# Turning the gathered rows in one piece, a group ahead, in the first stage of a four-layer graph network

## The chip, the cores and the metric

One Trainium2 chip, one of its cores. The time is device time in microseconds (us) of one execution of the whole program; shown are the median of several runs and one profiled execution. Engines: PE is TensorE, PEld its weight loads, DVE VectorE, ACT ScalarE, POOL GpSimd, SP the engine that issues most transfers.

## What is computed

A graph of 12,500 nodes with 32 features and 412,500 edges sorted by destination. Four layers, each followed by a layer norm over x plus the layer's output:

```python
# layer 0: an edge network, averaged over the edges of a node, then a node network
h = concatenate([x[src], edge_attr_16], axis=1)        # 48 wide
h = maximum(h @ w1a + b1a, 0.0)                        # 96 wide
h = h @ w1b + b1b
agg = segment_sum(h, dst) / maximum(count, 1)
x = layernorm(x + (maximum(concat([x, agg]) @ w2a + b2a, 0) @ w2b + b2b))
# layer 1: ten steps of normalised propagation, f = 0.9 * (A f) + 0.1 * f0
# layer 2: x = layernorm(x + A x)
# layer 3: messages from node features, edge directions and a radial network, summed by dst
```

A is the matrix of how many edges run from a node to another. The kernel builds it once, in the first stage, as counts in 8-bit floats, and layers 1 and 2 multiply by it.

## The kernel before

The nodes stand in NB = 98 blocks of 128, the edges in NG = 324 groups of 1280 (G = 10 tiles of 128). The change touches one stage alone, the function `edges_and_adjacency`, which does two things interleaved on all engines.

The first is layer 0's edge network. For each group POOL gathers the 1280 source rows with ten indirect DMAs into one of NX = 6 buffers `xin`, laid out edges by features. PE transposes each 128x32 tile into the bank `xt_ps` (features by edges, on 32 partitions), ACT copies that to `xt`, where the 16 edge attributes and a row of ones already stand below it. PE multiplies by `w1a` in two halves of five tiles (`hidden`), ACT applies the Relu to each half out of the same bank `h_ps`. Then, for each block of nodes that the group's destinations reach (the "visits", 1.3 a group on average, because the edges are sorted), DVE writes a one-hot matrix and PE sums the ten tiles into `e_visit_ps` with ten matmuls. The block numbers, first and end, are read on PE and on DVE from a table in SBUF (`blocks`, two `value_load`).

The second is the count matrix A. It is made in NQ = 56 quarters; in each, 56 pairs of node windows. A "pair" is four matmuls: for each of two windows one into `a_ps` (one of two banks, by the pair's parity) and one into `degree_ps`, from one-hot matrices `hot_hi` and `hot_lo` that DVE writes in batches of eight windows, four pairs, into two buffers. ACT casts each pair from `a_ps` to the fp8 `image`, and PE waits for `a_taken` of the pair two before. SP stores an image of a quarter in seven parts; ACT may write over an image when all seven of the older quarter are stored (`image_stored`). Once in a quarter PE also folds an image (49 matmuls) as a check.

After two quarters of pairs alone, a loop of 54 turns does a quarter of pairs and six groups (m = 0 to 5) each. DVE does 3, 2, 2, 3, 2, 2 batches ahead of a group's visits (`BATCHES`), so PE and ACT have 12, 8, 8, 12, 8, 8 pairs to place in a group. The order in a group is written out by hand, in the same order on PE and ACT: `STEPS_PAIRS` says how many pairs follow each step. Before the change the steps are: transposes of four tiles, of four, of two (`SUB`), each followed by 2 pairs; hidden half 0; hidden half 1; then 6 or 2 pairs; then the visits. Semaphores: `xt_ready` and `xt_evac` count three per group, POOL gathers into a buffer again when the three transposes of the group that used it are done, and SP loads the attributes of the group after next when the hidden matmuls (`h_ready`) and DVE's part of the visits (`group_read`) of this group are done.

Of the kernel before, what the change touches and what calls it, by code (L numbers as in the profile page):

```python
# [31 lines left out]
P = 128  # L32
# [60 lines left out]
def await_alone(eng, passed, sem, value):  # L93


    eng.wait_ge(sem, value)
    eng.sem_inc(passed, 1)
# [355 lines left out]
        nc.scalar.sqrt(var[:], var[:]).then_inc(root_ready, 1)  # L453


STEPS_PAIRS = ((2, 2, 2, 0, 6, 0), (2, 2, 2, 0, 2, 0))
BATCHES = (3, 2, 2, 3, 2, 2)
SUB = [(0, 4), (4, 4), (8, 2)]
HT = 5
M1 = DH + 1  # L460

# [1 line left out]
def edges_and_adjacency(nc, k, s):  # L463
# [16 lines left out]
    ones = sb("ones_col", [P, 1], F32, s)  # L480
    answer = sb("answer", [1, 4], F32, s)

    xt_ps = pb("xt_ps", [D, 512], F32, s)
    degree_ps = pb("degree_ps", [P, 512], F32, s)
    h_ps = pb("h_ps", [EP, 512], F32, s)
    visit_ps = pb("e_visit_ps", [M1, 512], F32, s)
# [18 lines left out]
    def blocks(eng, g):  # L505
        first = eng.value_load(k.table[0:1, 0, bass.ds(g, 1)], min_val=0, max_val=NB - 1)
        end = eng.value_load(k.table[0:1, 1, bass.ds(g, 1)], min_val=1, max_val=NB)
        return first, end

    with nc.Block() as block:  # L510

        @block.gpsimd
        def _(pool):
            with pool.Fori(1, NG // NX) as i:
                for m in range(NX):
                    await_alone(pool, k.passed_pool, k.idx_loaded[m], i * 16 + 16)
                    await_alone(pool, k.passed_pool, xt_ready, i * (3 * NX) + (3 * m + 3 - 3 * NX))
                    gather_group(k, pool, m)

        @block.sync  # L520
# [42 lines left out]
        @block.tensor  # L563
        def _(pe):
            def pairs(q, at, count):

                for l in range(at, at + count):
                    bank = l % 2
                    batch = l // 4
                    if l % 4 == 0:  # L570
                        pe.wait_ge(hot_ready, q * BPQ + (batch + 1))
                    pe.wait_ge(a_taken, q * QP + (l + 1))
                    for v in range(2):
                        w = l % 4 * 2 + v
                        lo = hot_lo[batch % 2][:, w, :]
                        counts = nc.tensor.matmul(a_ps[:, bank, v * WC:(v + 1) * WC], lo, hot_hi[batch % 2][:, w, :], start=True, stop=True)  # L576
                        mm = nc.tensor.matmul(degree_ps[:, 0:WC], lo, hot_hi[batch % 2][:, w, :], start=False, stop=False,  # L577
                                              skip_group_check=True)
                    counts.then_inc(a_ready, 1)
                    if l % 4 == 3:  # L580
                        mm.then_inc(hot_used, 1)

            def fold(q, n):

                pe.wait_ge(a_taken, q * QP + (QP + 2))
                await_alone(pe, k.passed_pe, folds_read, q + 1)
                for j in range(NB // 2):
                    strip = slice(j % 4 * D, (j % 4 + 1) * D)
                    mm = nc.tensor.matmul(check_ps[strip, 0:2 * QW], folded[:], image[:, n, 2 * j:2 * j + 2, :].bitcast(FP8),
                                          start=(j < 4), stop=(j >= NB // 2 - 4), tile_position=(0, j % 4 * D))  # L590
                mm.then_inc(folds_done, 1)

            def transposes(g, m, b):
                t0, tn = SUB[b]
                pe.wait_ge(xt_evac, g * 3 + (b + 1))
                for t in range(t0, t0 + tn):
                    mm = nc.tensor.transpose(xt_ps[:, (t - t0) * EP:(t - t0 + 1) * EP], xin[m][:, t, :], k.ident[:])  # L597
                mm.then_inc(xt_ready, 1)

            def hidden(g, m, b):  # L600
                pe.wait_ge(xt_evac, g * 3 + (3 + b))
                pe.wait_ge(h_evac, g * 2 + (b + 1))
                for t in range(HT):
                    mm = nc.tensor.matmul(h_ps[:, t * DH:(t + 1) * DH], xt[:, m % 2, (b * HT + t) * EP:(b * HT + t + 1) * EP], w1a[:],  # L604
                                          start=True, stop=True)
                mm.then_inc(h_ready, 1)

            def visits(g, m):
                pe.wait_ge(h_evac, g * 2 + 3)
                first, end = blocks(pe, g)  # L610
                with pe.Fori(first, end):
                    v = pe.snap(count, min_val=0, max_val=NG * NB)
                    pe.wait_ge(onehot_ready, v + 1)
                    pe.wait_ge(added, v + 2)
                    for j in range(G):
                        mm = nc.tensor.matmul(visit_ps[:, 0:P], hid[m % 2][:, j, :], view(onehot[:], (v % 2) * (G * P) + j * P, [[1, P]]),  # L616
                                              start=(j == 0), stop=(j == G - 1))
                    mm.then_inc(product_done, 1)
                    pe.reg_add(count, count, 1)

            def group(g, twos, m, turn, q, at):

                run = STEPS_PAIRS[BATCHES[m] == 2]
                pe.wait_ge(gathered[m], turn * (16 * G) + 16 * G)
                transposes(g, m, 0)
                pairs(q, at, run[0])
                transposes(g, m, 1)
                at += run[0]
                pairs(q, at, run[1])
                transposes(g, m, 2)  # L630
                at += run[1]
                pairs(q, at, run[2])
                at += run[2]
                pe.wait_ge(loaded[m % 2], twos * 32 + 32)
                hidden(g, m, 0)
                pairs(q, at, run[3])
                hidden(g, m, 1)
                at += run[3]
                pairs(q, at, run[4])
                at += run[4]  # L640
                visits(g, m)
                pairs(q, at, run[5])
                return at + run[5]

            pe.wait_ge(weights_loaded, 32)
            pe.wait_ge(zero_ready, 1)
            pe.wait_ge(folded_ready, 1)
            count = pe.alloc_register("e_visits_pe")
            pe.reg_mov(count, 0)
            nc.tensor.matmul(degree_ps[:, 0:WC], zero[0:1, 0:P], zero[0:1, 0:WC], start=True, stop=False, skip_group_check=True)  # L650
            nc.tensor.matmul(visit_ps[:, 0:P], zero[0:1, 0:M1], zero[0:1, 0:P], start=True, stop=True).then_inc(product_done, 1)
            pairs(0, 0, QP)
            pairs(1, 0, QP)
            fold(0, 0)
            with pe.Fori(0, NQ - 2) as u:
                at = 0
                for m in range(NX):
                    at = group(u * NX + m, u * (NX // 2) + m // 2, m, u, u + 2, at)
                    if m == 1:
                        odd = pe.snap(u % 2, min_val=0, max_val=1)  # L660
                        with pe.If(odd < 1):
                            fold(u + 1, 1)
                        with pe.If(odd > 0):
                            fold(u + 1, 0)
            fold(NQ - 1, 1)
            pe.wait_ge(verdict_ready, 1)
            nc.tensor.matmul(check_ps[0:1, 0:2], ones[:], verdict[:], start=True, stop=True).then_inc(verdict_turned, 1)

        @block.scalar
        def _(act):  # L670
# [8 lines left out]
                    nc.scalar.copy(view(image[:], h * (NB * QW) + 4 * l, [[QW, NB], [1, 4]]).bitcast(FP8),  # L679
                                   view(a_ps[:], l % 2 * 512, [[1, NB], [NB, 4]]), saturate=False).then_inc(a_taken, 1)  # L680

            def turned(g, m, b):
                t0, tn = SUB[b]
                act.wait_ge(xt_ready, g * 3 + (b + 1))
                nc.scalar.copy(xt[0:D, m % 2, t0 * EP:(t0 + tn) * EP],  # L685
                               xt_ps[:, 0:tn * EP]).then_inc(xt_evac, 1)

            def hidden(g, m, b):
                act.wait_ge(h_ready, g * 2 + (b + 1))
                nc.scalar.activation(hid[m % 2][:, b * HT:(b + 1) * HT, 0:DH], view(h_ps[:], 0, [[DH, HT], [1, DH]]),  # L690
                                     ACT.Relu).then_inc(h_evac, 1)

            def group(g, m, q, h, at):

                run = STEPS_PAIRS[BATCHES[m] == 2]
                turned(g, m, 0)
                pairs(q, h, at, run[0])
                at += run[0]
                turned(g, m, 1)
                pairs(q, h, at, run[1])  # L700
                at += run[1]
                turned(g, m, 2)
                pairs(q, h, at, run[2])
                at += run[2]
                hidden(g, m, 0)
                pairs(q, h, at, run[3])
                at += run[3]
                hidden(g, m, 1)
                pairs(q, h, at, run[4] + run[5])
                return at + run[4] + run[5]  # L710

            act.wait_ge(ones_ready, 1)
            pairs(0, 0, 0, QP)
# [1037 lines left out]
```

## Time and profile before

| what | value |
|---|---|
| median of 3 runs | 17071.12 us (17070.09 to 17088.16) |
| the profiled execution's own time | 17098.35 us |
| its span, first to last instruction | 17096.5 us |
| mean granted clock of TensorE | 0.891 |
| the changed stage, from the first transpose to the last visit | about 346 to 5775 us, 324 groups |

The page cuts the span into 40 slices of 427 us; slices 2 to 14 are the stage. A line of grouped instructions has the engine, the operation, what it writes and reads, how often, then busy time and mean ns of one, then the engine's idle time just before them and what ended it. "issue" means that nothing in the profile was waited for. In a timeline each line is a start, a length and in brackets the idle time before. A matmul's modelled end is late, so that consecutive ones overlap in the rows; from start to start is what one costs. A 4-byte matmul stands as two records.

### The profile page before, as it was taken

The numbers are of one execution on the slowest core, as the hardware profiler recorded it, in microseconds if no ns is written. First come the engines' busy times: TensorE is split into PE (matmuls) and PEld (weight loads), VectorE is DVE, ScalarE is ACT, GpSimd is POOL, SyncE is SP. The second block draws the span as 40 slices with busy tenths as digits, with TensorE's granted clock in tenths as the row PEclk, the third lists the DMA queues.
The fourth block names the chain that finished last, engine by engine and source line by source line (L and its number), as shares of the span: only waits on it lengthen the run. The fifth ranks groups of instructions, "written<-read, shape, count | busy, mean of one in ns | idle before, by whom it ended". The sixth has DMA issues, their size and how long they took to land. (4 is left out here: it accounts for less than half of the span.)

```text
span 17096.5 us, 397550 instructions
## 1 busy us (share of the span) xinstructions
PE 14417.9 (84%) x141860; PEld 9526.3 (56%) x141861; DVE 8838.1 (52%) x13201; ACT 5006.3 (29%) x10225; POOL 7476.6 (44%) x8530
## 2 busy tenths in 40 slices
PE   3888888888888769999999999878888888888887
PEld 2667677667766535555555555544444444444444
DVE  6555555555555421111011110128888888888888
ACT  2333333333333200000000000004444444444444
POOL 4555555555555100000000000017777777777776
PEclk9877777777777669999999999989999999999999
DMA  2111111111111039998999999861111111111111
GB/s 85 45 44 43 42 45 43 44 43 45 43 44 43 29 142 345 341 343 337 340 342 339 341 341 342 316 223 30 31 31 31 31 31 31 31 30 31 31 31 29
DMA packets 1140415, 2191.40 MB, mean 128 GB/s; under 512 B 399083, under 2 KB 506087, under 8 KB 1138759
## 3 DMA queue, kind: packets, MB, share of 16 engines
q1 hardware_dynamic: 928851, 2062.78, 33.7%
q0 software_dynamic: 210496, 113.01, 4.6%
q8 instruction: 837, 13.71, 0.3%
q14 instruction: 231, 1.89, 0.0%
HBM read 2002.85 MB, written 172.28 MB: 127 GB/s over the span
## 5 line engine op out<-in xcount | busy, mean ns | idle before, releaser
L1413 POOL DMA_INDIRECT m_src<-x_after_layer,m_idx x3240 | 3105.1, 958 | 6785.4 <-DMA m_idx<-in_src 5668.7
L1171 PE MATMUL p_prod<-a_slot,f_parts 128*32 128x448 fp8e4 x90552 | 4474.7, 360 | 392.0 <-issue 343.6
L175 POOL DMA_INDIRECT l_xin<-in_x,l_idx x3240 | 3068.0, 947 | 2476.5 <-DMA l_idx<-in_src 1268.3
L1171 PEld LDWEIGHTS p_prod<-a_slot,f_parts 128*32 128x32 bf16 x90552 | 2566.6, 99 | 2247.1 <-issue 586.7
L1544 PE MATMUL radial_ps<-radial_w,radial_hidden 128*128 128x384 f32 x6480 | 2459.6, 512 | 401.2 <-DVE m_products L1683 209.1
L1549 PE MATMUL m_visit_ps<-m_products,m_onehot 128*128 128x288 f32 x8420 | 2349.9, 427 | 456.2 <-DVE m_products L1702 239.2
L1264 DVE TENSOR_TENSOR agg<-agg,p_back 128x224 f32 x154 | 59.7, 388 | 4463.0 <-PE p_back L1185 4463.0
L1549 PEld LDWEIGHTS m_visit_ps<-m_products,m_onehot 128*128 128x128 f32 x8420 | 1599.7, 193 | 1226.9 <-issue 640.5
L1544 PEld LDWEIGHTS radial_ps<-radial_w,radial_hidden 128*128 128x128 f32 x6480 | 1140.0, 191 | 1630.2 <-DVE m_products L1683 759.5
L616 PE MATMUL e_visit_ps<-e_onehot,e_hidden 128*97 x8420 | 1581.8, 368 | 541.2 <-issue 480.2
L750 DVE TENSOR_TENSOR hot_hi<-window_hi,number_ps 128x1568 bf16<-128x1568 f32 x784 | 1399.9, 1786 | 1175.2 <-PE degree_ps L577 1114.1
L616 PEld LDWEIGHTS e_visit_ps<-e_onehot,e_hidden 128*97 128x97 f32 x8420 | 1472.4, 239 | 671.4 <-issue 671.4
L1683 DVE TENSOR_TENSOR m_products<-radial_ps,m_features 128x256 f32<-128x256 f32 x4860 | 1745.4, 415 | 0.0
L1224 ACT COPY turned<-p_prod 128x896 f32<-128x896 f32 x154 | 139.6, 906 | 5004.3 <-PEq L1178 5004.3
L576 PE MATMUL a_ps<-hot_hi,hot_lo 128*128 128x196 bf16 x6272 | 1461.7, 282 | 97.0 <-DVE hot_lo L752 88.3
L1516 ACT ACTIVATE m_difference<-m_nodes,m_dst 128x128 f32 x3240 | 982.1, 388 | 1884.7 <-PEq L1569 1884.7
L679 ACT CAST a_image<-a_ps 128x392 fp8e4<-128x392 f32 x3136 | 1404.6, 483 | 266.4 <-PE a_ps L576 236.5
L577 PE MATMUL degree_ps<-hot_hi,hot_lo 128*128 128x196 bf16 x6272 | 1459.7, 281 | 0.0
L1679 DVE TENSOR_TENSOR m_products<-radial_ps,m_features 128x512 f32<-128x512 f32 x1620 | 1113.1, 687 | 414.6 <-PE radial_ps L1544 296.4
L1499 ACT ACTIVATE radial_hidden<-edge_w,radial_w 64x1280 f32<-64x1280 f32 x324 | 874.7, 2700 | 1041.4 <-DMA m_unit<-edge_directions 904.1
L685 ACT COPY xt<-xt_ps 32x512 f32<-32x512 f32 (+1 forms) x972 | 491.0, 505 | 2315.4 <-PE xt_ps L597 2182.2
L604 PE MATMUL h_ps<-w1a,xt 49*128 49x96 f32 x6480 | 984.9, 302 | 213.7 <-ACT e_hidden L690 213.7
(197 smaller groups left out, 11894.1 us busy)
## 6 DMA issues: line engine op xcount, KB each, us to landing
a_slot<-multiplicity_digit SPq DMA_DIRECT2D x1078, 1568.0 KB, 9.3
multiplicity_digit<-a_image SPq DMA_DIRECT2D x392, 392.0 KB
edge_w<-in_edge_weight SPq DMA_DIRECT2D x324, 320.0 KB
l_xin<-in_x,l_idx POOLq DMA_INDIRECT x3240
m_src<-x_after_layer,m_idx POOLq DMA_INDIRECT x3240
xt<-in_edge_attr SPq DMA_DIRECT2D x324, 80.0 KB
edge_directions<-rel_unit SPq DMA_DIRECT2D x12, 675.0 KB, 3.8
m_unit<-edge_directions SPq DMA_DIRECT2D x324, 25.0 KB
```

The source lines that it names most:

```text
L175: pool.indirect_dma_start(k.xin[m][:, j, :], None, k.io["x"], bass.IndirectOffsetOnAxis(k.idx[m][:, j:j + 1], 0)).then_inc(k.gathered[m], 16)
L576: counts = nc.tensor.matmul(a_ps[:, bank, v * WC:(v + 1) * WC], lo, hot_hi[batch % 2][:, w, :], start=True, stop=True)
L577: mm = nc.tensor.matmul(degree_ps[:, 0:WC], lo, hot_hi[batch % 2][:, w, :], start=False, stop=False, skip_group_check=True)
L616: mm = nc.tensor.matmul(visit_ps[:, 0:P], hid[m % 2][:, j, :], view(onehot[:], (v % 2) * (G * P) + j * P, [[1, P]]), start=(j == 0), stop= ...
L679: nc.scalar.copy(view(image[:], h * (NB * QW) + 4 * l, [[QW, NB], [1, 4]]).bitcast(FP8), view(a_ps[:], l % 2 * 512, [[1, NB], [NB, 4]]), s ...
L750: tt(hot_hi[b % 2][:], view(k.window_hi[:, bass.ds(at, WB)], 0, [[1, WB], [0, WC]]), view(numbers, 0, [[0, WB], [1, WC]]), ALU.is_equal)
L1171: mm = nc.tensor.matmul(view(prod[m][rows, w, :], 0, [[QW, 2], [1, QW]]), source[:, h * HH + j, r * D:(r + 1) * D], slots[h][:, 2 * w:2 * ...
L1413: pool.indirect_dma_start(src[m][:, j, :], None, k.x3_d, bass.IndirectOffsetOnAxis(idx[m][:, j:j + 1], 0)).then_inc(gathered[m], 16)
L1544: mm = nc.tensor.matmul(r_ps[:, half, t, 0:RD], hid[m][:, b * RB + t, :], w2[:], start=True, stop=True)
L1549: mm = nc.tensor.matmul(view(v_ps[:], (v % 3) * 512, [[U + 1, D], [1, U + 1]]), onehot[one][:, j, :], view(prod[m][:], j * PW + FIRST, [[R ...
L1679: tt(view(prod[m][:], t0 * PW + 1, [[PW, RB], [RW, 2 * U], [1, 2 * U]]), view(r_ps[:], at, [[512, RB], [2 * U, 2 * U], [1, 2 * U]]), view( ...
L1683: mul = tt(view(prod[m][:], t0 * PW + LONG + o * U * RW + 1, [[PW, RB], [RW, U], [1, 2 * U]]), view(r_ps[:], at + 4 * U * U, [[512, RB], [ ...
```

## The change

In words: ten transposes of one 128x32 tile each, in three steps, become three transposes, of four, four and two tiles side by side (128, 128 and 64 columns of `xin`), into one bank of 128 partitions; tile t0 + place of each comes out on the 32 partitions of `place`. ACT brings them to `xt` with four copies, one for each set of 32 partitions, of 3, 3, 2 and 2 tiles. They are done for the group ahead: transposes of group g + 1 stand before the visits of g, its copies on ACT after the second run of pairs; only for m = 0, the first group of a turn, they stand at the group's own start. PE reads the block numbers after hidden half 0 and waits alone for the second Relu ahead of the visits. The pairs stand in three runs: 4 after half 0, 4 or 2 after half 1, 4 or 2 after the visits.

```diff
-STEPS_PAIRS = ((2, 2, 2, 0, 6, 0), (2, 2, 2, 0, 2, 0))
+STEPS_PAIRS = ((4, 4, 4), (4, 2, 2))
-SUB = [(0, 4), (4, 4), (8, 2)]
+WIDE = [(0, 4), (4, 4), (8, 2)]
...
-    xt_ps = pb("xt_ps", [D, 512], F32, s)
+    xt_ps = pb("xt_ps", [P, 512], F32, s)
...
-                    await_alone(pool, k.passed_pool, xt_ready, i * (3 * NX) + (3 * m + 3 - 3 * NX))
+                    await_alone(pool, k.passed_pool, xt_ready, i * NX + (m + 1 - NX))
...
-            def transposes(g, m, b):
-                t0, tn = SUB[b]
-                pe.wait_ge(xt_evac, g * 3 + (b + 1))
-                for t in range(t0, t0 + tn):
-                    mm = nc.tensor.transpose(xt_ps[:, (t - t0) * EP:(t - t0 + 1) * EP], xin[m][:, t, :], k.ident[:])
+            def transposes(g, m, turn):
+
+                pe.wait_ge(gathered[m], turn * (16 * G) + 16 * G)
+                pe.wait_ge(xt_evac, g + 1)
+                for i, (t0, tn) in enumerate(WIDE):
+                    mm = nc.tensor.transpose(xt_ps[0:tn * D, i * EP:(i + 1) * EP],
+                                             view(xin[m][:], t0 * D, [[1, tn * D]]), k.ident[:])
                 mm.then_inc(xt_ready, 1)
...
-            def visits(g, m):
-                pe.wait_ge(h_evac, g * 2 + 3)
-                first, end = blocks(pe, g)
+            def visits(g, m, first, end):
+                await_alone(pe, k.passed_pe, h_evac, g * 2 + 3)
...
-                pe.wait_ge(gathered[m], turn * (16 * G) + 16 * G)
-                transposes(g, m, 0)
-                pairs(q, at, run[0])
-                transposes(g, m, 1)
-                at += run[0]
-                pairs(q, at, run[1])
-                transposes(g, m, 2)
-                at += run[1]
-                pairs(q, at, run[2])
-                at += run[2]
+                if m == 0:
+                    transposes(g, m, turn)
                 pe.wait_ge(loaded[m % 2], twos * 32 + 32)
                 hidden(g, m, 0)
-                pairs(q, at, run[3])
+                first, end = blocks(pe, g)
+                pairs(q, at, run[0])
+                at += run[0]
                 hidden(g, m, 1)
-                at += run[3]
-                pairs(q, at, run[4])
-                at += run[4]
-                visits(g, m)
-                pairs(q, at, run[5])
-                return at + run[5]
+                pairs(q, at, run[1])
+                at += run[1]
+                if m < NX - 1:
+                    transposes(g + 1, m + 1, turn)
+                visits(g, m, first, end)
+                pairs(q, at, run[2])
+                return at + run[2]
...
-            def turned(g, m, b):
-                t0, tn = SUB[b]
-                act.wait_ge(xt_ready, g * 3 + (b + 1))
-                nc.scalar.copy(xt[0:D, m % 2, t0 * EP:(t0 + tn) * EP],
-                               xt_ps[:, 0:tn * EP]).then_inc(xt_evac, 1)
+            def turned(g, m):
+                act.wait_ge(xt_ready, g + 1)
+                for place in range(4):
+                    n = sum(place < tn for _, tn in WIDE)
+                    copied = nc.scalar.copy(view(xt[0:D, m % 2, :], place * EP, [[4 * EP, n], [1, EP]]),
+                                            view(xt_ps[place * D:(place + 1) * D, :], 0, [[EP, n], [1, EP]]))
+                copied.then_inc(xt_evac, 1)
```

ACT's `group` follows PE's new order: (m = 0: `turned`), Relu 0, run 0, Relu 1, run 1, `turned` of the group ahead, run 2. DVE and SP keep their programs.

## Rows read from the trace of the kernel before

**Rows 1.** The page: busy time, TensorE's clock in 40 slices, one 128-column weight load.

```profile
PE 14417.9 (84%) x141860; PEld 9526.3 (56%) x141861; DVE 8838.1 (52%) x13201; ACT 5006.3 (29%) x10225; POOL 7476.6 (44%) x8530
...
PEclk9877777777777669999999999989999999999999
...
L1544 PEld LDWEIGHTS radial_ps<-radial_w,radial_hidden 128*128 128x128 f32 x6480 | 1140.0, 191 | 1630.2 <-DVE m_products L1683 759.5
```

**Rows 2.** The windows view over the stage's middle: busy PE, PEld, DVE, ACT, POOL, clock, DMA.

```profile
380.00:5690.00 5310.00, 4504.18 (x32235) 3703.85 (x32234) 2884.29 (x2362) 2045.35 (x4549) 2994.00 (x3174) 0.77 0.17 44
```

**Rows 3.** The windows view, one group with one visit, cut into four stretches.

```profile
3311.93:3315.20 3.27, 2.61 (x21) 2.37 (x20) 2.56 (x2) 1.16 (x3) 2.53 (x3) 1.00 0.10 15
3315.20:3317.94 2.74, 0.87 (x9) 0.63 (x9) 1.72 (x2) 1.34 (x3) 2.13 (x3) 0.80 0.27 45
3317.94:3322.50 4.56, 4.56 (x21) 4.46 (x22) 1.20 (x2) 0.00 (x0) 3.34 (x5) 0.50 0.33 101
3322.50:3326.57 4.07, 4.07 (x35) 2.91 (x32) 1.02 (x1) 3.16 (x8) 3.15 (x4) 0.85 0.10 14
```

**Rows 4.** Groups of instructions by shape, 1000 to 5000 us, 239 groups of edges.

```profile
L175 POOL DMA_INDIRECT l_xin<-in_x,l_idx x2389 | 2253.7, 943 | 1746.1 <-DMA l_idx<-in_src 852.4 <-issue 672.0 <-PE xt_ps L597 221.7
L616 PE MATMUL e_visit_ps<-e_onehot,e_hidden 128*97 x6209 | 1174.9, 370 | 395.8 <-issue 350.5 <-DVE e_total L761 45.2
...
L679 ACT CAST a_image<-a_ps 128x392 fp8e4<-128x392 f32 x2230 | 999.2, 483 | 131.1 <-PE a_ps L576 108.9 <-issue 0.2
L750 DVE TENSOR_TENSOR hot_hi<-window_hi,number_ps 128x1568 bf16<-128x1568 f32 x556 | 992.9, 1786 | 872.6 <-PE degree_ps L577 827.5 <-issue 44.8
...
L752 DVE TENSOR_TENSOR hot_lo<-window_lo,number_ps 128x1024 bf16<-128x1024 f32 x556 | 675.2, 1214 | 0.0
...
L769 DVE SCALAR_TENSOR_TENSOR e_onehot<-e_dst,block_start,number_ps 128x1280 f32 x312 | 481.3, 1543 | 9.8 <-issue 9.8
...
L685 ACT COPY xt<-xt_ps 32x512 f32<-32x512 f32 x478 | 274.9, 575 | 1715.4 <-PE xt_ps L597 1615.4 <-DMA multiplicity_digit<-a_image 100.0
...
L685 ACT COPY xt<-xt_ps 32x256 f32<-32x256 f32 x239 | 87.3, 365 | 0.0
```

**Rows 5.** The waits view, 1000 to 5000 us: total, times, longest.

```profile
PE e_visit_ps L616 <- issue: 350.5, 238, 2.0
...
PE h_ps L604 <- ACT e_hidden L690: 157.7, 239, 0.7
```

**Rows 6.** Timeline: first transposes of a group to its first hidden half.

```profile
3004.80 0.61 PE L597 MATMUL xt_ps<-ident,l_xin 128*32 128x128 f32 x4
...
3005.25 0.25 PE L576 MATMUL a_ps<-hot_hi,hot_lo 128*128 128x196 bf16 x1
...
3005.42 0.25 PE L576 MATMUL a_ps<-hot_hi,hot_lo 128*128 128x196 bf16 x1
...
3008.56 1.35 PE L604 MATMUL h_ps<-w1a,xt 49*128 49x96 f32 x10
```

**Rows 7.** Timeline: second visit of a group; Relu 1, last pairs and visit of another.

```profile
3019.76 4.14 PE L616 MATMUL e_visit_ps<-e_onehot,e_hidden 128*97 x20 [0.63 <-DVE e_total L761]
...
3031.42 0.57 ACT L690 ACTIVATE e_hidden<-h_ps 128x480 f32<-128x480 f32 x1 [1.97 <-PE h_ps L604]
...
3034.93 0.37 PE L576 MATMUL a_ps<-hot_hi,hot_lo 128*128 128x196 bf16 x1
...
3036.96 4.08 PE L616 MATMUL e_visit_ps<-e_onehot,e_hidden 128*97 x20 [1.49 <-issue]
```

**Rows 8.** Timeline: last stores of a quarter, its last visit, the next turn's transposes.

```profile
3168.50 1.05 SPq L536 DMA_DIRECT2D multiplicity_digit<-a_image  x2
...
3169.24 4.49 PE L616 MATMUL e_visit_ps<-e_onehot,e_hidden 128*97 x20 [1.30 <-issue]
...
3173.57 0.60 PE L597 MATMUL xt_ps<-ident,l_xin 128*32 128x128 f32 x4
```

More of the change, by code:

```diff
@@ L591, in fold @@
                 mm.then_inc(folds_done, 1)
-            def transposes(g, m, b):
-                t0, tn = SUB[b]
-                pe.wait_ge(xt_evac, g * 3 + (b + 1))
-                for t in range(t0, t0 + tn):
-                    mm = nc.tensor.transpose(xt_ps[:, (t - t0) * EP:(t - t0 + 1) * EP], xin[m][:, t, :], k.ident[:])
+            def transposes(g, m, turn):
[4 more added lines that the diff above has]
+                                             view(xin[m][:], t0 * D, [[1, tn * D]]), k.ident[:])
                 mm.then_inc(xt_ready, 1)
             def hidden(g, m, b):
-                pe.wait_ge(xt_evac, g * 3 + (3 + b))
+                pe.wait_ge(xt_evac, g + 2)
                 pe.wait_ge(h_evac, g * 2 + (b + 1))
@@ L695, in group @@
                 run = STEPS_PAIRS[BATCHES[m] == 2]
-                turned(g, m, 0)
+                if m == 0:
+                    turned(g, m)
+                hidden(g, m, 0)
                 pairs(q, h, at, run[0])
                 at += run[0]
-                turned(g, m, 1)
+                hidden(g, m, 1)
                 pairs(q, h, at, run[1])
                 at += run[1]
-                turned(g, m, 2)
+                if m < NX - 1:
+                    turned(g + 1, m + 1)
                 pairs(q, h, at, run[2])
[L704 to L710, printed above, removed]
+                return at + run[2]
             act.wait_ge(ones_ready, 1)
```

## The prediction

> **What bounds the kernel now.** I read the page first, for where the changed stage lies and which engine is full there, then windows over the stage, then its groups of instructions and waits, then the timeline of single groups.
>
> The page gives whole-span shares that mix stages [rows 1]; the windows view is what counts. Over the stage's middle PE is busy 4504 of 5310 us (85%), DVE 54%, POOL 56%, ACT 39%, and the granted clock is 0.77 [rows 2]. So TensorE's in-order queue sets the pace, and the clock is part of it: 0.77 between the levels 2.4 GHz (1.0) and 1.2 GHz (0.5) means 46% of the time at the lower. 324 groups in 5429 us are 16.76 us each, 7.7 us of them at 1.2 GHz. The one group cut in four shows the pattern: full clock through transposes, pairs and the hidden halves, falling in the stretch with the few pairs and the idle before the visit, 1.2 GHz for the whole visit, back in the stretch after it [rows 3].
>
> Other engines, as floors for a group: POOL issues ten gathers of 0.943 us [rows 4] with 672.0/2201 = 0.31 us between, 12.5 us. DVE does 14 batches of 1.79 + 1.21 us in six groups and 1.3 one-hots of 1.54 us with an addition and drain of some 0.3 us, 9.4 us. Neither binds at 16.8 us; POOL would at 12.5.
>
> **The change part by part**, per group, at full clock unless said.
>
> *Transposes and their copies.* From the first transpose to hidden half 0 are 3.76 us [rows 6]. The 24 count matmuls in it start 0.17 us apart by twos, 0.085 each, 2.04 us. They stay (in other places), as does the 0.16 us ahead of the hidden half. The other 1.56 us, ten transposes and PE's short waits for ACT's copies between them, goes. Three transposes come, with 128, 128 and 64 columns to load as weights. No such form is in the stage. Bounds: 0.085 us each, as a transpose of one tile costs at most (0.26 in all), and 0.19 each as the 128-column 4-byte load [rows 1] (0.57). It is nearest to that load: 0.5. Gain 1.06; bounds 0.99 to 1.3. The second step of handing over, PE to ACT, is hidden behind visits of 2.1 us or more (20 records, 4.56 us at the lower clock [rows 3]): ACT needs 2 x 0.47 + 2 x 0.365 = 1.67 us for its four copies, 0.47 read between the copies of 256 and 512 elements, 0.365 and 0.575 [rows 4]. Before, it took 1.52, so ACT is as busy as it was.
>
> *Block numbers.* PE idles 350.5 us in 239 groups ahead of visits with no one to blame, 1.47 each, up to 2.0 [rows 5]. That this is not the Relu is seen where Relu 1 ended at 3031.99, the last pairs at about 3035.5 and the visit began at 3036.96 [rows 7]: the two table reads start only when the queue has passed the last pair. What stays is the loop's set-up: between nothing and the 0.63 us between two visits of a group, of which DVE's addition is part [rows 7]. I take 0.3: gain 1.17.
>
> *The same reads between the halves.* Before, PE stood 0.66 us after half 0 for the Relu (157.7/239 [rows 5]). That wait goes, the Relu lies behind 4 pairs. The reads stand in its place. Their whole length is up to 2.0; half 0 (1.35 us) runs meanwhile if PE's sequencer issues it and goes on. Lower bound 0 idle, upper 2.0. The rows before the visit show that the reads begin near the end of issued work, not long before; half 0 is longer work with no wait inside, so I take 0.8. Then 0.1 ahead of half 1 for a semaphore. Cost 0.8 + 0.1 - 0.66 = 0.25; bounds -0.6 to 1.4.
>
> In sentences that the sum does not need: the Trainium skill, "TensorE: Matmul & The Clock Gate", section "Architectural detail: the array is 16× 32×32, not 1× 128×128", gives TensorE a queue 64 entries deep. By that the reads would be issued under half 0 and the idle be near nothing, which is the third rival below. The trace did not show such depth ahead of a visit [rows 7], but there waits for casts stand inside the pairs, so it doesn't refute the page.
>
> *Runs of four pairs.* ACT casts a pair in 0.483 us [rows 4]; PE makes one in 4 x 0.085 = 0.34, with two banks. Runs of two never hit that at full clock; in a run of four, pairs 3 and 4 wait for casts 1 and 2. After half 0, with Relu 0 over, that is 2 x (0.48 - 0.34) and a semaphore, 0.4. At 1.2 GHz a pair takes 0.68 and it is nothing. Cost 0.4; the second run of four (m = 0, 3) would add 0.7 with Relu 1 in front at full clock, 0 at the lower, which I expect there.
>
> Sum so far: 1.06 + 1.17 - 0.25 - 0.4 = 1.58 a group, 9.5 a turn of six.
>
> *m = 0.* Here nothing hides the copies: transposes, 1.67 us of copies and two handovers of 0.2 stand between two hidden matmul streams. 2.1 us a turn. ACT may start them only when the seven stores of an older quarter have landed. Today the last two are issued up to 3169.55, 4.0 us ahead of the next transposes [rows 8]. They wait for `h_ready` and `group_read` of m = 5; both come about when half 1 ends, as before, and the visit and two pairs lie between: at the lower clock 0, at full some 1.4. I take 0.1.
>
> *One-hots of m = 0 and 3.* The third batch needs the buffer of the first, free after run 0. Then 3.0 us of batch and 1.54 of one-hot, 4.7 with handovers; PE has half 1, four pairs, transposes: 1.35 + 1.36 + 0.5 = 3.2 with no stall of its own, 5.9 at the lower clock. Cost 0 to 1.5 each, I take 0.25: 0.5 a turn. With 2 batches the one-hot depends on the pairs of the previous group's end, 4.9 us after which it is ready, and PE needs it after 6.5. DVE was a group ahead, and now is just in time: that cover is gone.
>
> Nothing for the pairs after the visits, SP's queue (the same five issues), or POOL, whose gathers are released earlier.
>
> Total: 9.5 - 2.1 - 0.1 - 0.5 = 6.8 us a turn; 54 turns give 367 us. 17098.35 - 367 = 16731 for the profiled execution; the median stands 27 us below that, so 17071 - 367 = 16704. The clock I leave at its share: the hidden halves, with their 49-row operand, and idle still come once a group, and it fell there each time.
>
> **The rivals.**
>
> *The clock holds.* Hidden halves are now split by four pairs and the idle before the visit is gone; before, only two pairs stood in 5.4 us of hidden work and idle, and the clock fell there. If it no longer falls, the 7.7 us a group at 1.2 GHz shrink, by up to 3 us. POOL's 12.5 us and DVE's chain then stop it. Halfway, 1.5 us a group, gives 486 us more, 16220. For it: the clock's pattern [rows 3]. Against it: PE's activity at each hidden half is low, and one fall costs the whole next visit. Chance 0.15.
>
> *The clock stays down.* (Slower.) The fast stretch was transposes and six pairs in dense order. It is broken up into 4, 2 and 2 pairs between hidden halves; at m = 0 a 2.1 us hole is added. If TensorE doesn't recover after a visit, 8 to 12 pairs cost 0.34 more each, half 0 and transposes 0.7: 3 us lost against 1.13 (6.8/6) won. It decides where 38% of groups stay down throughout; at 60%, 3 x 0.6 - 1.13 = 0.67 a group, 217 us: 17290. In the profile before, the clock came back after each visit. Chance 0.10.
>
> *The reads are hidden wholly under half 0.* 0.8 x 324 = 259 more: 16445. It is the queue's depth. Chance 0.15.
>
> *The reads only move.* Idle between the halves is the full 2.0 instead of 0.8: 389 us less, 17090, no gain. The change then doesn't do what it says. For it: the row where the reads start no earlier than the last pair [rows 7]. Chance 0.06.
>
> **How the numbers follow.** My case, 16704, has 0.54, and by its bounds (transposes +-0.2, visits +-0.3, casts and one-hots +-0.3 a group) its own range is 16500 to 16900. The rivals have 0.15, 0.10, 0.15 and 0.06. The range for 8 in 10 leaves out most of the first (below 16340) and the slow ones above 17000: 16340 to 17000. A measurement of this kernel tells 0.2%, 34 us, from no change. Faster by more: 0.54 + 0.15 + 0.15 and a third of the fourth rival, 0.86; within: 0.04; slower: 0.10.
>
> **What the changed profile would show.** Right: PE's idle ahead of visits with "issue" falls from 1.47 to about 0.3 us a group; PE no longer waits for Relu 0, but idles some 0.8 us between half 0 and pairs; three transposes take 0.5 us; four ACT copies 1.67; before m = 0's half 0 PE stands 2 us; the stage lasts about 5060 us at a clock of 0.75 to 0.80; other stages take the same. Wrong: a clock above 0.85 or below 0.72, a large new wait of visits for the one-hot, of transposes for gathers, or of the first copies for stores.

## The result and the profile after

The changed kernel takes 15895.33 us (median of 4 runs, 15881.43 to 15908.74) against 17077.57 us before: a ratio of 0.9301, 95% interval 0.9289 to 0.9313, 1182 us less. The forecast of 16704 (16340 to 17000) had the sign and a third of the size.

The page of the kernel after, busy time and the clock in 40 slices of 397 us (the stage is slices 2 to 11):

```profile
PE 13338.8 (84%) x139592; PEld 8678.4 (55%) x139593; DVE 8833.2 (56%) x13201; ACT 5096.5 (32%) x10549; POOL 7479.4 (47%) x8530
...
PEclk8999999999967999999999999899999999999999
```

Windows over the stage's middle, after, answering to [rows 2], then one group with one visit, answering to [rows 3], cut at half 1, at the visit and at the pairs behind it (columns as there):

```profile
380.00:4350.00 3970.00, 3414.45 (x29815) 2867.73 (x29808) 2863.18 (x2345) 2117.47 (x4829) 2972.05 (x3150) 0.94 0.23 58
...
2506.95:2510.18 3.23, 2.98 (x28) 2.38 (x27) 2.86 (x4) 1.62 (x4) 2.32 (x4) 1.00 0.10 12
2510.18:2512.77 2.59, 2.46 (x22) 2.10 (x22) 2.38 (x2) 1.80 (x5) 1.98 (x3) 1.00 0.11 13
2512.77:2515.03 2.26, 2.26 (x21) 2.25 (x21) 0.54 (x1) 1.68 (x5) 1.77 (x2) 1.00 0.58 155
2515.03:2515.80 0.77, 0.77 (x10) 0.61 (x8) 0.00 (x0) 0.23 (x1) 0.65 (x1) 1.00 0.61 232
```

The clock rose from 0.77 to 0.94. This group never leaves 2.4 GHz: its visit takes 2.26 us, where the one before took 4.56 [rows 3]. From the first transpose to the last visit the trace has 4086 us, 12.61 a group, against 5429 and 16.76: 1343 us less. What follows the stage takes 11448 us against 11322, 126 us more; that is why the whole gains less. PE's own idle fell from (5310 - 4504.18)/317 = 2.5 us a group [rows 2] to (3970 - 3414.45)/315 = 1.8.

Groups of instructions, after, 1000 to 4300 us (262 groups of edges, against 239 in [rows 4]):

```profile
L175 POOL DMA_INDIRECT l_xin<-in_x,l_idx x2617 | 2469.4, 944 | 830.9 <-issue 782.3 <-DMA l_idx<-in_src 47.4 <-PE xt_ps L598 1.2
...
L675 ACT CAST a_image<-a_ps 128x392 fp8e4<-128x392 f32 x2440 | 1084.4, 488 | 811.8 <-PE a_ps L576 738.2 <-issue 57.0
...
L617 PE MATMUL e_visit_ps<-e_onehot,e_hidden 128*97 x6819 | 833.7, 278 | 167.4 <-DVE e_total L756 129.4 <-issue 22.5
...
L682 ACT COPY xt<-xt_ps 32x384 f32<-32x384 f32 x524 | 245.6, 469 | 98.3 <-issue 56.8 <-DMA multiplicity_digit<-a_image 34.1 <-PE xt_ps L598 4.1
L682 ACT COPY xt<-xt_ps 32x256 f32<-32x256 f32 x524 | 191.9, 366 | 6.1
...
L598 PEld LDWEIGHTS xt_ps<-ident,l_xin 128*128 128x128 f32 x524 | 62.4, 147 | 0.4
```

Waits of PE in the same stretch (total, times, longest), answering to [rows 5]:

```profile
PE h_ps L606 <- ACT xt L682: 182.4, 44, 5.3
PE e_visit_ps L617 <- DVE e_total L756: 129.4, 139, 1.4
...
PE a_ps L576 <- ACT a_image L675: 90.3, 364, 0.3
...
PE e_visit_ps L617 <- issue: 22.5, 56, 0.5
```

"issue" ahead of visits fell from 350.5 us in 239 groups to 22.5 in 262. No wait for the Relu is left, nor any idle in its place: in the timeline of that group the pairs start as half 0 ends.

```profile
2506.95 1.35 PE L606 MATMUL h_ps<-w1a,xt 49*128 49x96 f32 x10
...
2508.24 0.26 PE L576 MATMUL a_ps<-hot_hi,hot_lo 128*128 128x196 bf16 x1
...
2512.15 0.49 PE L598 MATMUL xt_ps<-ident,l_xin 128*128 128x128 f32 x3
...
2512.77 2.42 PE L617 MATMUL e_visit_ps<-e_onehot,e_hidden 128*97 x20
2512.78 1.71 ACT L682 COPY xt<-xt_ps 32x384 f32<-32x384 f32 x4
```

The four copies (1.71 us) lie behind the visit. And POOL, idle for 44% of the time before [rows 4], now has hardly any room: 2469.4 us busy, 782.3 us between gathers with nothing awaited, and 48.6 us of waits make 3300 us of 3300.

### The profile page after: what moved, and what is told of

The parts are those of the page before. It is cut to its first block and busy times, and to the rows that moved or that the text cites. A ratio compares the mean times of both kernels' runs of the same rounds, so it can differ in the third digit from the quotient of the medians.

```text
span 15879.6 us, 392042 instructions
## 1 busy us (share of the span) xinstructions
PE 13338.8 (84%) x139592; PEld 8678.4 (55%) x139593; DVE 8833.2 (56%) x13201; ACT 5096.5 (32%) x10549; POOL 7479.4 (47%) x8530
## 5 line engine op out<-in xcount | busy, mean ns | idle before, releaser
L576 PE MATMUL a_ps<-hot_hi,hot_lo 128*128 128x196 bf16 x6272 | 1322.6, 263 | 179.2 <-ACT a_image L675 118.2
L577 PE MATMUL degree_ps<-hot_hi,hot_lo 128*128 128x196 bf16 x6272 | 1314.0, 260 | 0.0
L617 PE MATMUL e_visit_ps<-e_onehot,e_hidden 128*97 x8420 | 1028.1, 278 | 206.4 <-DVE e_total L756 159.3
L617 PEld LDWEIGHTS e_visit_ps<-e_onehot,e_hidden 128*97 128x97 f32 x8420 | 945.7, 166 | 301.8 <-issue 300.8
L606 PEld LDWEIGHTS h_ps<-w1a,xt 49*128 49x128 f32 x6480 | 848.1, 204 | 348.7 <-issue 348.7
```

## The experiments

The question was what lifted the clock, and what else limits. "Stage" is first transpose to last visit in each trace. Each ratio is to runs of the kernel before that were taken beside the experiment (medians 17078 to 17093 us). Theory A is that the pairs between the hidden halves hold the clock, theory B that the idle ahead of the visit let it fall.

| kernel | time, us | ratio to before, 95% | stage, us | its clock |
|---|---|---|---|---|
| before | 17077.57 | | 5429 | 0.77 |
| changed | 15895.33 | 0.9289 to 0.9313 | 4086 | 0.94 |
| e1 changed, reads late | 16343.1 | 0.9556 to 0.9588 | 4537 | 0.92 |
| e2 changed, no pairs between halves | 16499.92 | 0.9646 to 0.9678 | 4679 | 0.87 |
| e3 before, reads moved | 16430.94 | 0.9603 to 0.9635 | 4760 | 0.84 |
| e4 before, pairs moved | 16674.66 | 0.9744 to 0.9776 | 4980 | 0.92 |
| e5 before, both moved | 16226.39 | 0.9482 to 0.9517 | 4536 | 0.94 |
| e6 changed, code shifted | 15782.61 | 0.9214 to 0.9245 | 4077 | 0.94 |
| e7 all groups ahead | 15770.76 | 0.9206 to 0.9237 | 4024 | 0.95 |
| e8 as e7, nine gathers | 15565.62 | 0.9095 to 0.9126 | 3833 | 0.98 |
| e9 changed, none ahead | 17205.31 | 1.0050 to 1.0083 | 5382 | 0.76 |
| e10 as e7, code shifted | 15699.52 | 0.9169 to 0.9199 | 4011 | 0.96 |
| e11 before, code shifted | 17121.03 | 1.0010 to 1.0029 | 5404 | 0.78 |

**e1_reads_late.** The reads go back to where they were.

```diff
                 hidden(g, m, 0)
-                first, end = blocks(pe, g)
                 pairs(q, at, run[0])
...
-            def visits(g, m, first, end):
+            def visits(g, m):
                 await_alone(pe, k.passed_pe, h_evac, g * 2 + 3)
+                first, end = blocks(pe, g)
```

> The changed kernel with one thing undone: PE reads the block numbers after the wait for Relu 1, ahead of the visits, as before the change. Theory A (the pairs between the hidden halves hold the clock): the idle of 1.2 to 1.9 us before the visit returns, 324 x 1.5 = 490 us, the stage's clock stays near 0.9, time about 16400. Theory B (the idle ahead of the visit was what let the clock fall): idle returns and the stage's clock falls to about 0.8, another 600 to 900 us, time about 17000.

451 us more in the stage, 1.39 a group, of which 1.11 is the idle ahead of visits (315.7 us in 264 groups), and the clock at 0.92. Windows over its stage, and PE's wait ahead of visits:

```profile
380.00:4820.00 4440.00, 3556.09 (x30010) 3010.07 (x30009) 2882.28 (x2360) 2107.19 (x4862) 2993.02 (x3173) 0.92 0.21 52
```
```profile
PE e_visit_ps L618 <- issue: 315.7, 184, 2.0
```

Theory A holds here: the price is mostly the idle, and little the clock.

**e2_none_between.**

```diff
-STEPS_PAIRS = ((4, 4, 4), (4, 2, 2))
+STEPS_PAIRS = ((0, 8, 4), (0, 6, 2))
```

> The changed kernel with the pairs taken out from between the hidden halves: runs of 0, 8, 4 and 0, 6, 2. Theory A: hidden half, wait for Relu 0, hidden half stand together again, the stage's clock falls to 0.8 or below and the time rises to about 16700. Theory B: the clock stays above 0.9; only the 0.66 us wait for Relu 0 returns, 210 us, less the casts' stalls: about 16050.

16500, between the two expectations. The clock fell to 0.87, so the pairs between the halves do hold it, though not alone.

```profile
380.00:4940.00 4560.00, 3731.67 (x29921) 3099.52 (x29919) 2871.96 (x2352) 2179.82 (x4846) 2980.74 (x3160) 0.87 0.20 51
```

**e3_old_reads_moved.** The kernel before with e1's edit reversed.

```diff
                 hidden(g, m, 0)
+                first, end = blocks(pe, g)
                 pairs(q, at, run[3])
```

> The kernel before with the block numbers read after hidden half 0 and nothing else. Theory A: the idle before the visit (1.47 us) goes but for 0.3, of which nothing comes back between the halves as PE waits there for Relu 0 anyway (0.66 us); clock unchanged at 0.77: 324 x 1.1 = 360 us less, 16700. Theory B: the clock rises to about 0.9 as well: about 16000.

669 us less, 2.06 a group, at 0.84. Both theories miss: the idle ahead of visits fell by 1.33 us, from 1.47 to 36.5/266 = 0.14, and the wait for Relu 0 stayed (0.66 us a group). The other 0.7 us is what is left for the clock, as a difference; the time at the lower level fell from 7.7 to 0.32 x 14.7 = 4.7 us a group, in which the lost idle lies too.

```profile
380.00:5020.00 4640.00, 4205.56 (x32130) 3476.51 (x32130) 2861.90 (x2353) 2031.65 (x4531) 2983.05 (x3162) 0.84 0.20 50
```
```profile
PE h_ps L604 <- ACT e_hidden L690: 175.5, 266, 0.7
...
PE e_visit_ps L615 <- issue: 36.5, 104, 0.5
```

**e4_old_pairs_moved.**

```diff
-STEPS_PAIRS = ((2, 2, 2, 0, 6, 0), (2, 2, 2, 0, 2, 0))
+STEPS_PAIRS = ((2, 2, 0, 4, 4, 0), (2, 0, 0, 4, 2, 0))
```

> The kernel before with only the pairs moved: 4 of them between the hidden halves (2, 2, 0, 4, 4, 0 and 2, 0, 0, 4, 2, 0). Theory A: the 0.66 us wait goes, waits for the transposes' copies come (up to 1 us), and the clock rises to 0.9: about 16200. Theory B: idle before the visit stays, clock stays near 0.77, time within 150 us of 17077.

The clock rose to 0.92 as theory A has it, with the whole idle ahead of the visit in place and even longer (448.1 us in 260 waits, 1.72 each). The time is some 410 us below before, not the 880 expected: PE now stands for the transposes' copies (132.2 us), as four or two pairs are left among them, not six, and the idle costs what it did.

```profile
380.00:5240.00 4860.00, 3938.37 (x32173) 3245.68 (x32172) 2870.05 (x2356) 2003.94 (x4539) 2988.69 (x3169) 0.92 0.19 48
```
```profile
PE e_visit_ps L616 <- issue: 448.1, 260, 1.9
...
PE xt_ps L597 <- ACT xt L685: 132.2, 187, 2.2
```

**e5_old_both_moved.** e3 and e4 in one kernel.

> The kernel before with both moves together: block numbers read between the halves, and 4 pairs there; transposes stay ten, in three steps, in their own group. If the two effects on time add, as the single moves measured (669 and 449 us of the stage's 5429), the stage takes 4310 us, at a clock near 0.93. What is then left to the changed kernel's 4086 us, some 220 us or 0.7 us a group, is the transposes' part. Rival: the two share one gain (both fill the same slow stretch), then the stage stays near 4700 us, and the transposes are worth 600 us.

4536 us, between the two expectations of 4310 and 4700: the two are worth 893 together, not 1118, so they share 225. The clock is where the changed kernel has it, 0.94, with all ten narrow transposes in place; so fewer transposes are not what lifted it. What is left for the rest of the change is 450 us, 1.39 a group: the wide transposes, their place a group ahead, and the pairs that stand behind the visits instead of among the transposes. These three were not taken apart in full; e9 undoes the second alone.

**e9_wide_in_place.** The wide transposes and their copies stand at the start of their own group.

```diff
-                if m == 0:
-                    transposes(g, m, turn)
+                transposes(g, m, turn)
...
-                if m < NX - 1:
-                    transposes(g + 1, m + 1, turn)
```

(and the same two for ACT's `turned`).

> The changed kernel with the three wide transposes and their copies at the start of their own group for every m, as it has them for m = 0: reads and pairs as in the changed kernel. If hiding the copies behind the visits is what the transposes' part is worth, each of 270 groups gets a bare wait of about 2.1 us (1.7 us of copies and two handovers; no stores to wait for), 570 us, and the clock falls from 0.94 to about 0.90 by the new hole: stage 4700 to 4850 us. If the narrower instruction count is what helps, the stage stays within 200 us of 4086.

Far worse than either expectation: 17205 us, 0.7% slower than before. PE waits 584.7 us in 265 groups for the copies, 2.2 each, against 182.4/262 = 0.70 in the changed kernel; the stage costs 4.0 us a group more. The other 2.5 are put down to the clock, at 0.76: 0.48 x 16.6 = 8.0 us a group at the lower level against 1.5 are 3.2 us by its halving, less what of it was idle.

```profile
380.00:5640.00 5260.00, 4325.98 (x29953) 3631.76 (x29954) 2875.04 (x2354) 2234.62 (x4856) 2988.75 (x3169) 0.76 0.18 44
```
```profile
PE h_ps L606 <- ACT xt L679: 584.7, 265, 5.0
```

In its timeline, transposes, copies, then half 0 after a bare 1.92 us; the 1.35 us matmuls of a half take 2.08:

```profile
3006.48 0.49 PE L598 MATMUL xt_ps<-ident,l_xin 128*128 128x128 f32 x3
...
3007.06 1.70 ACT L679 COPY xt<-xt_ps 32x384 f32<-32x384 f32 x4
...
3008.89 2.08 PE L606 MATMUL h_ps<-w1a,xt 49*128 49x96 f32 x10 [1.92 <-ACT xt L679]
```

**e7_all_ahead.** The last group of a turn does the first of the next.

```diff
-                if m == 0:
-                    transposes(g, m, turn)
...
                 if m < NX - 1:
                     transposes(g + 1, m + 1, turn)
+                else:
+                    more = pe.snap(turn, min_val=0, max_val=NQ)
+                    with pe.If(more < NQ - 3):
+                        transposes(g + 1, 0, turn + 1)
```

> The changed kernel with the first group of each turn transposed a group ahead too (the last group of a turn does it; the very first group ahead of the loop). PE's wait of 4.1 us for ACT's copies once a turn goes. Theory P (PE still sets the pace): 54 x 4 = 216 us less, stage 3870 us. Theory G (the gathers on POOL, 12.5 us a group, are now the floor, PE at 12.6): stage not below 318 x 12.5 = 3975 us less what the gathers are ahead (42 us), 3930 to 4000 us, and PE shows a new wait ahead of the transposes.

4024 us, close to theory G and far from P. A new wait stands ahead of the transposes, for the gathers, and POOL waits for nothing but its own issue:

```profile
POOL l_xin L175 <- issue: 780.4, 2559, 0.3
...
PE xt_ps L598 <- DMA l_xin<-in_x,l_idx: 127.8, 94, 4.1
```

**e8_all_ahead_nine.** It gathers nine of the ten tiles of a group after the first six groups, and the waits for gathers count nine; the tenth tile keeps the rows of an earlier group, so this is a measurement and no kernel to use.

```diff
-                    gather_group(k, pool, m)
+                    gather_group(k, pool, m, G - 1)
```

> The kernel of the run before with nine gathers a group instead of ten after the first six groups (the tenth tile keeps the rows of an earlier group). POOL's floor becomes 11.2 us a group. Theory G: the stage falls further, by up to 1 us a group, 100 to 300 us. Theory P: the stage takes what it took with ten gathers, within 20 us.

191 us less in the stage, and the wait for gathers is gone; POOL now waits for indices. The gathers are the floor of e7, 12.4 to 12.5 us a group, and the changed kernel's 12.6 stand just above it.

```profile
POOL l_xin L175 <- issue: 676.7, 2201, 0.9
...
POOL l_xin L175 <- DMA l_idx<-in_src: 158.7, 89, 4.6
```

**e6_padded.** 112 instructions on PE, once, ahead of the later stage's loops.

```diff
             def _(pe):
+                for _ in range(112):
+                    pe.sem_inc(k.passed_pe, 1)
                 planes = pe.value_load(k.ctl[0:1, 1:2], min_val=1, max_val=DIGITS)
```

> The changed kernel with 112 semaphore increments that nobody waits for on PE, once, ahead of the loops of the later stage that multiplies by A (PE's code ahead of it is 112 instructions shorter after the change). Theory: that stage's 120 us loss comes from where the loop's code lies; moved back, its rounds take 464 us again instead of 476, and the time falls by 110 us to 15780. Rival: the loss has to do with something else (the data, the clock); nothing changes but 6 us more for the increments.

As the theory had it: 113 us less with the stage nearly unchanged (4077). A round, one pass of the later stage over A, takes 465.8 us (mean of the first nine); 476.4 in the changed kernel, 464.4 before. Where PE lost them is seen in the waits over most of that stage, of before (5000 us), changed (5140 us) and shifted (5040 us), one fence each. The stalls come about every 67 us, at the turns of the inner loop, with nothing awaited: 4.9 us each before, in the changed kernel 7.9 or 5.0 and 1.7 together:

```profile
PE p_prod L1171 <- issue: 338.3, 96, 41.7
```
```profile
PE p_prod L1166 <- issue: 464.3, 105, 41.8
```
```profile
PE p_prod L1168 <- issue: 357.2, 109, 41.7
```

**e10_all_ahead_padded** is e7 with 98 increments, **e11_before_padded** the kernel before with 112.

> Every group's transposes a group ahead, and 98 semaphore increments that bring the later stage's loop on PE back to the place it had before the change. Stage 4024 us as without them, rounds of the later stage 464 to 466 us instead of 471: 60 us less than the 15771 without them, 15710. Rival (code place is not it): 15770.

15699.52, rounds of 465.6: as expected, and faster than the changed kernel by 196 us and than the kernel before by 1378.

> The kernel before with 112 such increments on PE ahead of the later stage. If the place of the loop's code sets the cost, moving it the other way by as much changes the rounds too: they become 470 to 480 us against 464, the time 17150 to 17200. If the changed kernel's loss had another cause, the time is that of before plus 6 us.

Too much expected: rounds of 466.2, the time up 0.2%. The place matters, but the loss is not the same in both directions. The other traces agree, and rule out the first stage's speed or clock as the cause: e1, e2 and e9, which have the changed kernel's transposes and no increments, have rounds of 476 to 478; e3, e4 and e5, with the ten narrow ones, 464 to 466, though e5's first stage is as fast as e1's; e7, whose code is 98 instructions short instead of 112, has 471. What about the place does it (a boundary in memory, how code is fetched) was not tried.

## Why the prediction was wrong

**The step that failed** is "The clock I leave at its share". The stage ran at 0.94, and a clock above 0.85 was the first sign of being wrong that I had named. Between clocks of 0.77 and 0.94 the time at the lower level fell from 0.46 x 16.76 = 7.7 us to 0.12 x 12.61 = 1.5 us a group. Had PE worked all through it, that is worth 3.1 us; the whole gain of the stage is 4.15, the sum gave 1.13. I argued that the hidden halves with their 49-row operand and the idle still come once a group. They do (PE still idles 1.8 us a group), but what stood beside them decided: e4 put pairs between the halves and changed no idle before the visit, and the clock went to 0.92; e3 took only that idle and got 0.84; e9 made one hole of 2.2 us a group, right ahead of half 0, and got 0.76. I had this as the first rival and stopped it halfway, at 16220 and 0.15. It went nearly all the way, to POOL's floor of 12.5 us, which that rival names. With the terms below at their measured sizes the sum comes to some 2.0 us a group, so about 2.2 of the 4.15 are the clock's (an estimate), nearly three quarters of the 3.0 that the sum missed; the terms are the rest.

**Terms of the sum.** *Transposes*: 1.06 expected. A 128-column transpose has a weight load of 0.147 us, and three start to start take about 0.3, not 0.5, which makes 1.56 - 0.3 = 1.26. I took 0.085 us as the most that a narrow one costs; [rows 6] has four in 0.45 us, 0.11 each, and a wide one costs the same 0.11. The 1.39 a group from e5 to the changed kernel do not measure this term, as e5 waits for copies too (150.4 us in 3000, 0.7 a group). *Ahead of visits*: the idle without cause fell by 1.38, 1.17 expected. *Reads between the halves*: expected to idle PE for 0.8, they cost nothing, and the wait for Relu 0 (0.66) went. That was the third rival, with 0.15; it came true beside the first. In the group shown above PE's sequencer starts the two reads 0.85 us ahead of half 0's first matmul (2506.95) and just at it, and the first pair follows at 2508.24 (the source views of the two lines):

```profile
L506 PEldq TENSOR_LOAD <-block_table x1: 299/299/299, 2506.1 to 2506.1; - x1
...
L507 PEldq TENSOR_LOAD <-block_table x1: 299/299/299, 2506.9 to 2506.9; - x1
```

The Trainium skill's queue of 64 entries ("TensorE: Matmul & The Clock Gate", section "Architectural detail: the array is 16× 32×32, not 1× 128×128") fits what is seen: with no wait inside half 0, PE's sequencer passes it early enough to hide both reads. No run here measures the depth. *Runs of four*: 0.34 us a group of wait for casts, 0.4 expected. *One-hots*: with the additions 129.4/262 = 0.49 us a group, against 45.2/239 = 0.19 before. I had 0.08 more for a clock that would be low there; at full clock the bound was 0.5.

**m = 0** was mis-sized: 4.1 us a turn, not 2.1 + 0.1. ACT stands 2.1 us on average ahead of its copies (56.8 + 34.1 us in 44 turns), by two causes that alternate:

```profile
ACT xt L682 <- issue: 56.8, 20, 3.3
...
ACT xt L682 <- DMA multiplicity_digit<-a_image: 34.1, 24, 3.0
```

On the turns in the middle of ACT's loop, which holds two turns in one pass, it waits for the stores of the older quarter, 1.4 us each, and starts 0.18 us after the last has landed. On the turns where that loop starts anew the wait is 2.8 us and ends with nothing that the profile names. In the turn below SP issues the last stores just after the visit starts (2468.09); their last landing event in the trace is at 2472.43, 0.7 us after ACT and the transposes are ready, and the copies start 1.9 us after it:

```profile
2468.92 0.97 SPq L536 DMA_DIRECT2D multiplicity_digit<-a_image  x2
...
2471.02 0.49 PE L598 MATMUL xt_ps<-ident,l_xin 128*128 128x128 f32 x3
...
2474.36 1.71 ACT L682 COPY xt<-xt_ps 32x384 f32<-32x384 f32 x4 [2.60 <-issue]
```

e9 has the same 22 waits of 2.5 us with "issue" (55.8 us), though its stores wait less (11.6 us). So there are two misses: for the stores I had 0 to 1.4 by the clock, and took the low clock's value; the start of ACT's loop, which nothing hides now, I had not priced at all. Why it takes that long was not tried.

**Not foreseen**: 120 us in a stage whose code did not change, by its place. I wrote that other stages take the same.

**The slower rival** was near: e9 is this change with only the look-ahead left out, its clock stays down and it is slower than before by 0.7%. The reason was the hole in every group, though; breaking up the dense stretch, which that rival feared, left the changed kernel at 0.94.

## What to carry to other kernels

Where TensorE's clock is below its full level in a stage, price a change by what it does to the thin stretches and idle, before pricing instructions: 1.5 us more of bare wait a group cost 4 here (e9), and moving dense matmuls between two thin streams was worth 593 us of the changed kernel's stage (e2) where removing a wait was worth 451 (e1), and 449 against 669 in the kernel before (e4, e3). When a busy engine gets faster, write down the floors of the others first; here the change met the gathers' 12.5 us, and after it hiding the largest wait of TensorE that was left (e7) gained less than 1%. Compare the stages that did not change, too: the loss there was a tenth of the gain.

## What was not expected of the hardware

The granted clock answered to holes of 2.2 us on average (1.92 in the timeline shown) beside hidden halves of 49 rows: 0.76 with one in every group (e9), 0.94 with one in a turn. The Trainium skill, in "TensorE: Matmul & The Clock Gate", section "Loop structure matters more than you think", says that the loop nest decides whether matmuls stay warm; its example has a much longer wait, and the rows here show it for short ones. How the chip weighs idle against a thin operand is left open.

With a PE program 112 instructions shorter ahead of a large loop, each of eleven passes through it took some 12 us longer, without a wait on any semaphore; 112 increments brought 10.6 us of them back.
